# Weights of a quantised feed-forward prepared beside the attention's keys; the attention's tail and the feed-forward each in one run

## The chip, the cores and the metric

The kernel runs on one core of a Trainium2 chip. The time is that of the device for one execution, in microseconds (us). Engines: PE (TensorE), DVE (VectorE), ACT (ScalarE), POOL (GpSimd), and SP, which issues the DMAs.

## What is computed

`x` has 16 x 128 tokens of 256 elements. It passes through four layers, each an attention on a second sequence and a feed-forward; the change is in layer 2:

```python
x = x + tanh(g_xattn[2]) * L2_xattn(layernorm(x), ctx, Wq, bq, Wkv, bkv, Wp, bp)
x = x + tanh(g_ffn[2])   * L2_ffn(layernorm(x), W1, b1, W2, b2, s_act1, s_act2)

# L2_xattn: 16 heads of 16; q, k quantised to +-127 per head and token, v per channel over all tokens
#   (scale sv = max|v| / 127); p = softmax(q k^T) quantised to 0..255 per row; out = (p v) @ Wp + bp
# L2_ffn: W1 is 1024 x 256, W2 is 256 x 1024
sw1, sw2 = max|W1| / 7, max|W2| / 7
x_q  = clip(round(x / s1), -8, 7) * s1
W_q  = clip(round(W / sw), -8, 7) * sw        # for W1 and W2
b1_q, b2_q = round(b1 / (s1*sw1)) * (s1*sw1), round(b2 / (s2*sw2)) * (s2*sw2)
h_q  = clip(round(relu(x_q @ W1_q^T + b1_q) / s2), 0, 15) * s2
out  = h_q @ W2_q^T + b2_q
```

## The kernel before

Everything stays in SBUF: `X` and `H` hold the residual and its normalised form, 128 tokens by 16 tiles (t) by 256; `hT` holds the transposed form. The layers are written one behind the other. Within a layer each engine has its own program, and the engines meet at semaphores only; between layers all engines meet at a barrier. An engine works its program in order, so whatever stands behind a wait waits too. Rounding is done by adding and subtracting a large constant, MAGIC.

The quantised attention, `quantised_attention`, has four parts.

1. `run(NormTransposed, LoadSplit)`, 1281 to 1308: layer norm and transposition of x, and the split of the context and of the weights wq, wk, wv and wp into an f16 high and low part (ACT copies, DVE subtracts, L1034 and L1039).
2. A block for keys, values and queries, 1308 to 1413. SP issues four small loads (biases); DVE waits for all of them. PE projects 16 key tiles into two PSUM banks, and DVE adds the bias in tile after tile (L2068). POOL adds gate x bp to all of X in one instruction (L1953). Then PE projects the values, which ACT evacuates (L2020), while DVE makes the keys' integers; then the queries in the same way (L2075), the values' integers, and the queries' integers, with transpositions by PE and ACT between. The value scales `sv`, one for each of the 256 channels, lie across partitions; SP writes them to DRAM and reads them back in broadcast form as `svb`.
3. The main loop over 256 pairs of a tile and a head, 1413 to 2173: scores on PE, maxima on DVE, exp on ACT, a DMA transposition, a cast on POOL, the weighted sum on PE. It leaves unscaled outputs in `H` and the row sums in `sums`.
4. The tail. `Transposed` with `ScaledOutputs`: DVE sums, takes the reciprocal and, for each pair of tiles, multiplies by it (L2267), multiplies by `svb` (L2274) and subtracts the high part (L461); ACT makes the high part and copies; PE transposes in f16 (L502); ACT and DVE evacuate. When all of it is done `OutProjection` runs: six matmuls of 256 columns for a tile, two banks, and DVE adds each tile to X (L2301).

The feed-forward, `quantised_ffn`, has two blocks. In the first SP loads both weights, 1 MB each, and the small vectors; DVE does the layer norm (L94 to L104), the largest magnitudes of both weights (L2396), the input's integers (L2401 to L2403), the scales and biases (L2405 to L2417), and the weights' integers in three passes each (L2420 to L2422). POOL takes the maximum across partitions (L2380) and adds gate x b2 to X (L2382). PE and ACT transpose the integers. In the second block, four times for 512 tokens: eight times a hidden product (L2438), ReLU with scale and bias on ACT (L2468), rounding in two steps on DVE (L2489, L2491) with two buffers each; when all eight are there, 32 matmuls for the output (L2454) and two additions to X on DVE (L2479).

Of the kernel before, what the change touches and what calls it, by code (L numbers as in the profile page):

```python
# [14 lines left out]
P = 128  # L15
NB = 16
# [1868 lines left out]
def quantised_attention(nc, sh, a, gate):  # L1885
# [13 lines left out]
    with ExitStack() as ctx:  # L1899
# [11 lines left out]
        svb = sb("svb", [P, D])  # L1911
# [3 lines left out]
        with ExitStack() as inner:  # L1915
            cT = sb("cT", [P, 2, KT * T], F16, inner)
            wq, wk, wv = (sb(x, [P, 2, KT * D], F16, inner) for x in ("wq", "wk", "wv"))
            with ExitStack() as head:
                items = [(cT, a["ctxT"]), (wq, a["qa_wq"]), (wk, a["qa_wk"]), (wv, a["qa_wv"]), (wp, a["qa_wp"])]
                run(nc, NormTransposed(nc, head, sh, "qa_hT"), LoadSplit(nc, head, items, "qa_load"))  # L1920
            Y = sb("Y", [P, NB, D], F32, inner)
            Z = sb("Z", [P, NB, D], F32, inner)
            stack = sb("stack", [P, NB, NH, SLOT], F16, inner)
            ints = sb("ints", [P, KT, T], BF16, inner)
            amax = sb("amax", [P, NB, NH], F32, inner)
            sv = sb("sv", [P, KT], F32, inner)
            rsv = sb("rsv", [P, KT], F32, inner)
            s_b, s_b4, s_mmk, s_mmq, s_mmv, s_evk, s_evq, s_evv, s_c, s_st, s_st1, s_st2, s_vi, s_Tk, s_Tq, s_Tv, s_tk, s_tq, s_tv, s_sv, s_out, s_in = map(sem, (
                "bias", "b4", "mmk", "mmq", "mmv", "evk", "evq", "evv", "chain", "st", "st1", "st2", "vi", "Tk", "Tq", "Tv", "tk", "tq", "tv", "sv", "svout", "svin"))
# [3 lines left out]
            sv_dram = nc.dram_tensor("qa_value_scales", [P, KT], F32, kind="Internal").ap()  # L1933
# [4 lines left out]
            with nc.Block() as block:  # L1938
                @block.sync
                def _(sp):  # L1940
# [64 lines left out]
                def _(act):  # L2005
# [9 lines left out]
                    act.wait_ge(s_b, 64)  # L2015
# [13 lines left out]
                    transposed(KT, lambda t: V[:, t, :].rearrange("p (m c) -> p m c", m=KT), s_Tv, s_tv)  # L2029
                    act.wait_ge(s_st1, 1)  # L2030
# [5 lines left out]
                def _(dve):  # L2036
# [27 lines left out]
                    dve.wait_ge(s_b, 64)  # L2064
# [181 lines left out]
class ScaledOutputs:  # L2246
# [29 lines left out]
    def scalar(self, act):  # L2276
        pass
# [1008 lines left out]
```

## Time and profile before

| | |
|---|---|
| three runs | 2568.63, 2575.75, 2576.99 us; median 2575.75 |
| the profiled execution | 2577.9 us |
| its span (first to last instruction) | 2576.2 us |
| head of the attention (norm, split) | 1281 to 1308 |
| keys, values, queries | 1308 to 1413 |
| main loop | 1413 to 2173 |
| tail | 2173.6 to 2214.8 |
| feed-forward, preparation | 2216.1 to 2261.0 |
| feed-forward, products | 2261.0 to 2312.6 |
| next layer's attention | 2313 to 2471 |
| next layer's ternary feed-forward | 2471.4 to the end |

All times of the profile are us from the start of the span. A row of a stretch gives how long each engine was busy in it and how many instructions began there; PEclk is the clock that PE was granted, as a share of 2.4 GHz, so 0.50 is the lower of its two levels, 1.2 GHz. A row of a group takes together the instructions of one line, engine and shape. PE's ends are modelled, and a busy PE need not be one at its peak.

### The profile page before, as it was taken

The numbers are of one execution on the slowest core, as the hardware profiler recorded it, in microseconds if no ns is written. First come the engines' busy times: TensorE is split into PE (matmuls) and PEld (weight loads), VectorE is DVE, ScalarE is ACT, GpSimd is POOL, SyncE is SP. The second block draws the span as 40 slices with busy tenths as digits, with TensorE's granted clock in tenths as the row PEclk, the third lists the DMA queues.
The fourth block names the chain that finished last, engine by engine and source line by source line (L and its number), as shares of the span: only waits on it lengthen the run. The fifth ranks groups of instructions, "written<-read, shape, count | busy, mean of one in ns | idle before, by whom it ended". The sixth has DMA issues, their size and how long they took to land. (4 is left out here: it accounts for less than half of the span.)

```text
span 2576.2 us, 51573 instructions
## 1 busy us (share of the span) xinstructions
PE 2065.3 (80%) x17553; PEld 1136.7 (44%) x17553; DVE 1827.0 (71%) x3580; ACT 1523.3 (59%) x2785; POOL 888.5 (34%) x795
## 2 busy tenths in 40 slices
PE   4867999999978868999756788888888885357856
PEld 1334656555645635887433233333333332224433
DVE  4776755555555587333565999999999998866865
ACT  3455533333356755333334899999999997144555
POOL 4730000000015523001310667777777774105401
PEclk8778999999989979999866555555555555687989
DMA  6351222222240072322200454554444443001101
GB/s 194 84 222 61 68 66 66 65 69 65 66 134 27 3 270 58 67 67 63 79 22 2 78 91 91 91 92 93 92 91 91 91 93 64 35 20 47 28 1 34
DMA packets 384505, 195.75 MB, mean 76 GB/s; under 512 B 312443, under 2 KB 355835, under 8 KB 382203
## 3 DMA queue, kind: packets, MB, share of 16 engines
q1 hardware_dynamic: 381245, 184.87, 28.9%
q0 software_dynamic: 3072, 8.39, 1.0%
q8 instruction: 116, 1.90, 0.3%
q14 instruction: 72, 0.59, 0.1%
HBM read 95.38 MB, written 23.09 MB: 46 GB/s over the span
## 5 line engine op out<-in xcount | busy, mean ns | idle before, releaser
L2212 ACT ACTIVATE qa_e<-qa_S,qa_nb,qa_sq 128x512 uint8<-128x512 f32 (+1 forms) x805 | 710.5, 892 | 15.1 <-DVE qa_nb L2227 9.0
L2223 DVE TENSOR_REDUCE qa_mx<-qa_S 128x1 f32<-128x512 f32 x1024 | 637.2, 683 | 25.7 <-PE qa_S L2178 23.1
L2178 PE MATMUL qa_S<-qa_kT,qa_qb 128*128 128x512 f16 x1024 | 536.5, 612 | 114.3 <-ACT qa_e L2212 102.9
L2154 POOL CAST qa_pT<-qa_eT 128x2048 bf16<-128x2048 uint8 x256 | 483.7, 1892 | 210.4 <-DMA qa_eT<-qa_e 157.9
L2178 PEld LDWEIGHTS qa_S<-qa_kT,qa_qb 128*128 128x128 f16 x1024 | 89.9, 106 | 455.9 <-ACT qa_e L2212 440.6
L1116 POOL MEMSET rms_nothing<- 128x512 f16 x1 | 0.5, 524 | 580.3 <-POOLq L3177 580.3
L973 PE MATMUL moe_G<-hT,moe_W 128*128 (+1 forms) x792 | 193.8, 381 | 7.1 <-DVE moe_zero L941 7.1
L982 PE MATMUL moe_O<-moe_W,moe_ap 128*128 (+1 forms) x1584 | 194.5, 273 | 4.1 <-DVE moe_ap L937 4.1
L913 ACT ACTIVATE moe_ap<-moe_a 128x512 f16<-128x512 f32 x132 | 83.4, 632 | 193.4 <-DVE moe_a L935 193.4
L2187 PEld LDWEIGHTS qa_O<-qa_V,qa_pT 128*128 128x128 bf16 x4096 | 162.4, 107 | 75.0 <-issue 67.1
L973 PE MATMUL moe_U<-hT,moe_W 128*128 (+1 forms) x792 | 193.0, 380 | 0.0
L982 PEld LDWEIGHTS moe_O<-moe_W,moe_ap 128*128 128x128 f16 x1584 | 154.7, 98 | 50.4 <-DVE moe_ap L937 3.9
L932 DVE TENSOR_TENSOR moe_t<-moe_sg,moe_wb 128x512 f32<-128x512 f32 x132 | 91.4, 693 | 111.8 <-ACT moe_sg L908 107.3
L2187 PE MATMUL qa_O<-qa_V,qa_pT 128*128 128x16 bf16 x4096 | 158.0, 177 | 7.1 <-POOL qa_pT L2154 7.1
L2212 ACT ACTIVATION_READ_ACCUMULATOR qa_e<-qa_S,qa_nb,qa_sq 128x1 f32 x805 | 161.1, 200 | 0.0
L908 ACT ACTIVATE moe_sg<-moe_G 128x512 f32<-128x512 f32 x132 | 78.9, 598 | 132.3 <-PE moe_G L973 132.1
L937 DVE TENSOR_TENSOR moe_ap<-moe_a,moe_ap 128x512 f16<-128x512 f32 x132 | 91.4, 693 | 92.0 <-ACT moe_ap L913 92.0
L1704 DVE TENSOR_TENSOR moe_a<-moe_GU,moe_sg 128x512 f32<-128x512 f32 x78 | 53.9, 690 | 116.1 <-PE moe_GU L1779 88.0
L1779 PE MATMUL moe_GU<-moe_xs,moe_W 128*128 128x256 f16 x1104 | 130.0, 275 | 5.0 <-issue 5.0
L1588 ACT ACTIVATE moe_ap<-moe_a 128x512 f16<-128x512 f32 x78 | 49.3, 632 | 121.8 <-DVE moe_a L1704 115.5
L973 PEld LDWEIGHTS moe_U<-hT,moe_W 128*128 (+1 forms) x792 | 77.7, 98 | 94.1 <-issue 1.3
L1779 PEld LDWEIGHTS moe_GU<-moe_xs,moe_W 128*128 x1104 | 109.0, 99 | 18.6 <-issue 5.2
(432 smaller groups left out, 3433.7 us busy)
## 6 DMA issues: line engine op xcount, KB each, us to landing
moe_wb<-weights_T SPq DMA_DIRECT2D x264, 128.0 KB, 2.8
moe_W<-in_moe_w SPq DMA_DIRECT2D x40, 384.0 KB, 11.3
moe_W<-in_moe_w SPq DMA_DIRECT2D x11, 1152.0 KB, 14.8
moe_xs_rows<-rms_nothing SPq DMA_DIRECT2D x46, 128.0 KB, 1.9
moe_ys_rows<-moe_ys SPq DMA_DIRECT2D x23, 256.0 KB, 2.1
conv_rows<-conv_parts SPq DMA_DIRECT2D x16, 256.0 KB, 3.4
qa_eT<-qa_e SPq DMA_TRANSPOSE x256, 3.0
conv_qst<-conv_rows SPq DMA_DIRECT2D x96, 32.0 KB
```

Of the source, the lines that this page charges most:

```text
L908: nc.scalar.activation(sg[:, u, :], G[:, u, :], ACT.Silu).then_inc(s_sg[u], 1)
L913: nc.scalar.activation(ap[:, u, 0, :], a[:, u, :], ACT.Copy).then_inc(s_hi[u], 1)
L932: nc.vector.tensor_tensor(t1[:, u, :], sg[:, u, :], wb[:, u, :], ALU.mult).then_inc(s_t1[u], 1)
L937: nc.vector.tensor_tensor(ap[:, u, 1, :], a[:, u, :], ap[:, u, 0, :], ALU.subtract).then_inc(s_lo[u], 1)
L973: last = nc.tensor.matmul(X_[:, u, :], sh.W[:, f, wp, base + k * P:base + (k + 1) * P], sh.hT[:, xp, k, bass.ds(c * CT, CT)], start=i == 0 ...
L982: last = nc.tensor.matmul(O[:, t, :], ap[:, u, xp, t * P:(t + 1) * P], sh.W[:, f, wp, 4 * P:TW], start=False, stop=False, skip_group_check ...
L1779: last = nc.tensor.matmul(out[:, half * SLOT_TILE:(half + 1) * SLOT_TILE], W[:, bass.ds(f, 1), wp, base + k * P:base + (k + 1) * P], xs[:, ...
L2154: nc.gpsimd.tensor_copy(pT[:, u % RING, :, :].rearrange("p (b r) q -> p b r q", r=2), pairs).then_inc(s_cast, 1)
L2178: nc.tensor.matmul(S[:, bank(m), :], qb[:, g // 2, j, g % 2, :], kT[:, g, q * QW:(q + 1) * QW], start=True, stop=True).then_inc(s_S, 1)
L2187: last = nc.tensor.matmul(O[:, h * HD:(h + 1) * HD], pT[:, u % RING, b, :], V[:, b, h * HD:(h + 1) * HD], start=b == 0, stop=b == NB - 1)
L2212: nc.scalar.activation(e8[:, u % RING, q * QW:(q + n) * QW], S[:, b:b + n, :].rearrange("p b c -> p (b c)"), ACT.Exp, bias=nb[:, u % 2:u % ...
L2223: nc.vector.reduce_max(mx[:, i, q:q + 1], S[:, bank(m + q), :], axis=AXX).then_inc(s_mx, 1)
```

## The change

The weights of the feed-forward get a class of their own, `QuantisedWeights`, whose buffers live through both layers. SP loads them in the attention's second block, behind one more load, `wpf`, the f32 output weights, which `LoadSplit` no longer takes. DVE works on the feed-forward's weights in pieces between the evacuations of the key tiles: magnitudes behind tiles 1 and 2, scales behind 5, the three passes of W1 behind 6 to 8 and of W2 behind 9 to 11, b1 and b2 behind 12 and 13. POOL takes their maximum behind its addition to X. The value scales are multiplied into the rows of `wpf` (there each channel is a partition), and the high and low part of `wp` are made from that; `svb` and its way through DRAM are gone.

The tail becomes one block, `scaled_projection`: POOL multiplies the tiles by the reciprocals, PE transposes pairs in f32, ACT makes the high part from PSUM and DVE the low part, PE projects, DVE adds a pair to X at once; transposes run two pairs ahead of projections.

`quantised_ffn` becomes one block: statistics by quarters of four tiles, ACT normalises with 1/s1 in the scale, DVE makes the integers of a quarter in two operations, and 32 steps of a hidden product (two ahead), ReLU, rounding and that product's four matmuls to the output. b2 enters PSUM by f32 matmuls of one row of ones with `b2`, in place of the addition on POOL. All loops are written out. The diff, cut:

```diff
+    def greatest(self, pool):
+        pool.wait_ge(self.s_am, 2)
+        self.nc.gpsimd.partition_all_reduce(self.amx[:, :], self.am[:, :], P, bass.bass_isa.ReduceOp.max).then_inc(self.s_amx, 1)
...
+    def magnitudes(self, dve, i):
+        if i == 0:
+            dve.wait_ge(self.s_load, 96)
+        self.nc.vector.tensor_reduce(out=self.am[:, i:i + 1], in_=(self.f1, self.f2)[i][:, :], axis=AXX, op=ALU.max,
+                                     apply_absolute_value=True).then_inc(self.s_am, 1)
...
+    def divided(self, dve, i):
+        f = (self.f1, self.f2)[i]
+        self.chained(self.nc.vector.tensor_scalar(f[:, :], f[:, :], self.rsw[:, i:i + 1], MAGIC, ALU.mult, ALU.add))
+    def rounded(self, dve, i):
+        f = (self.f1, self.f2)[i]
+        self.chained(self.nc.vector.tensor_scalar(f[:, :], f[:, :], MAGIC, 7.0, ALU.subtract, ALU.min))
+    def integers(self, dve, i):
+        f, w = (self.f1, self.f2)[i], (self.w1, self.w2)[i]
+        self.nc.vector.tensor_scalar(w[:, :], f[:, :], -8.0, None, ALU.max).then_inc(self.s_w, 1)
...
-                    sp.wait_ge(s_sv, 1)
-                    sp.dma_start(sv_dram, sv[:, :]).then_inc(s_out, 16)
-                    sp.wait_ge(s_out, 16)
-                    sp.dma_start(svb[:, :], sv_dram.rearrange("p m -> (p m)").partition_broadcast(P)).then_inc(s_in, 16)
-                    sp.wait_ge(s_in, 16)
+                    sp.dma_start(wpf[:, :], a["qa_wp"]).then_inc(s_b, 16)
+                    next_weights.load(sp)
...
+                    next_weights.greatest(pool)
...
+                    act.wait_ge(s_wps, KT)
+                    nc.scalar.activation(wp[:, 0, :], wpf[:, :], ACT.Copy).then_inc(s_wphi, 1)
...
-                    dve.wait_ge(s_b, 64)
+                    dve.wait_ge(s_b, 80)
...
+                    next_weights.start(dve)
+                    for t in range(NB):
+                        dve.wait_ge(s_mmk, t + 1)
+                        nc.vector.tensor_tensor(Y[:, t, :], QP[:, t % 2, 0:D], bias[:, 1, :], ALU.add).then_inc(s_evk, 1)
+                        if t in (1, 2):
+                            next_weights.magnitudes(dve, t - 1)
+                        if t == 5:
+                            next_weights.scales(dve, next_gate)
+                        if t in (6, 9):
+                            next_weights.divided(dve, (t - 6) // 3)
+                        if t in (7, 10):
+                            next_weights.rounded(dve, (t - 7) // 3)
+                        if t in (8, 11):
+                            next_weights.integers(dve, (t - 8) // 3)
+                        if t == 12:
+                            next_weights.hidden_bias(dve)
+                        if t == 13:
+                            next_weights.output_bias(dve)
+                    dve.wait_ge(s_evk, NB + 2)
...
+                    for m in range(KT):
+                        nc.vector.tensor_scalar(wpf[:, m * D:(m + 1) * D], wpf[:, m * D:(m + 1) * D], sv[:, m:m + 1], None, ALU.mult).then_inc(s_wps, 1)
...
+                    dve.wait_ge(s_wphi, 1)
+                    nc.vector.tensor_tensor(wp[:, 1, :], wpf[:, :], wp[:, 0, :], ALU.subtract)
...
+            @block.gpsimd
+            def _(pool):
+                pool.wait_ge(s_inv, 1)
+                for t in range(NB):
+                    h = sh.H[:, t, :].rearrange("p (h d) -> p h d", h=heads)
+                    nc.gpsimd.tensor_tensor(h, h, inv[:, t, :].unsqueeze(2).to_broadcast([P, heads, D // heads]), ALU.mult).then_inc(s_scaled, 1)
...
+                def low(p):
+                    dve.wait_ge(s_hi, p + 1)
+                    nc.vector.tensor_tensor(target(1, p), turned(p), target(0, p), ALU.subtract).then_inc(s_lo, 1)
...
+                nc.vector.reciprocal(inv[:, :, :].rearrange("p t h -> p (t h)"), tot[:, :]).then_inc(s_inv, 1)
+                low(0)
+                low(1)
+                for p in range(PAIRS):
+                    if p + 2 < PAIRS:
+                        low(p + 2)
+                    residual(p)
...
+                def transposes(p):
+                    pe.wait_ge(s_scaled, 2 * p + 2)
+                    if p >= 3:
+                        pe.wait_ge(s_lo, p - 2)
...
+                def project(p):
+                    pe.wait_ge(s_lo, p + 1)
+                    if p >= 3:
+                        pe.wait_ge(s_res, p - 2)
...
+                transposes(0)
+                transposes(1)
+                for p in range(PAIRS):
+                    if p + 2 < PAIRS:
+                        transposes(p + 2)
+                    project(p)
...
+                def hidden(n):
+                    q, f = divmod(n, NF)
+                    pe.wait_ge(s_hT, q + 1)
+                    if n >= RING:
+                        pe.wait_ge(s_r, n - RING + 1)
...
+                def biases(q):
+                    if q >= 2:
+                        pe.wait_ge(s_res, 2 * (q - 1))
+                    for i in range(Q):
+                        nc.tensor.matmul(O[:, q % 2, i, :], ones[0:1, :], b2[0:1, :], start=i % 2 == 0, stop=False, skip_group_check=True)
+                def down(n):
+                    q, f = divmod(n, NF)
+                    pe.wait_ge(s_hq, n + 1)
+                    for i in range(Q):
+                        last = nc.tensor.matmul(O[:, q % 2, i, :], hq[:, n % 4, i * P:(i + 1) * P], w2[:, f * D:(f + 1) * D],
+                                                start=False, stop=f == NF - 1, skip_group_check=True)
+                    last.then_inc(s_D, 1)
...
+                tokens(0)
+                hidden(0)
+                hidden(1)
+                biases(0)
+                for n in range(NQ * NF):
+                    q, f = divmod(n, NF)
+                    if f == 2 and q + 1 < NQ:
+                        tokens(q + 1)
+                    if f == 5 and q + 1 < NQ:
+                        biases(q + 1)
+                    if n + 2 < NQ * NF:
+                        hidden(n + 2)
+                    down(n)
...
+                for q in range(NQ):
+                    deviations(q)
+                    if q < 2:
+                        for t in range(q * Q, (q + 1) * Q):
+                            normalise(t)
+                tokens(0)
+                for n in range(NQ * NF):
+                    q, f = divmod(n, NF)
+                    if f == 3 and q + 1 < NQ:
+                        tokens(q + 1)
+                    relu(n)
+                    if f % 2 == 0 and q + 2 < NQ:
+                        normalise((q + 2) * Q + f // 2)
...
+                def rounded(n):
+                    dve.wait_ge(s_r, n + 1)
+                    nc.vector.tensor_scalar(z[:, n % 2, :], r[:, n % RING, :], 15.0, MAGIC, ALU.min, ALU.add).then_inc(s_z, 1)
+                    dve.wait_ge(s_z, n + 1)
+                    if n >= 4:
+                        dve.wait_ge(s_D, n - 3)
+                    nc.vector.tensor_scalar(hq[:, n % 4, :], z[:, n % 2, :], MAGIC, None, ALU.subtract).then_inc(s_hq, 1)
...
+                statistics(0)
+                statistics(1)
+                scales(0)
+                statistics(2)
+                scales(1)
+                integers(0)
+                statistics(3)
+                scales(2)
+                scales(3)
+                for n in range(NQ * NF):
+                    q, f = divmod(n, NF)
+                    rounded(n)
+                    if f == 0 and q + 1 < NQ:
+                        integers(q + 1)
+                    if f == 3 and q:
+                        output(q - 1)
+                output(NQ - 1)
```

## Rows read from the trace of the kernel before

**Rows 1.** Stretches: length, busy us (instructions) per engine, clock, DMA share, GB/s

```profile
1313.20:1328.40 15.20, 13.43 (x88) 9.23 (x89) 7.24 (x18) 0.00 (x0) 8.84 (x1) 0.78 0.01 1
1328.40:1355.70 27.30, 11.14 (x58) 5.44 (x56) 26.66 (x11) 5.51 (x8) 0.00 (x0) 0.78 0.00 0
...
1369.80:1397.70 27.90, 15.79 (x94) 9.42 (x93) 27.49 (x15) 16.87 (x33) 0.00 (x0) 0.58 0.07 5
1413.00:2173.00 760.00, 638.50 (x5126) 228.61 (x5125) 722.72 (x1552) 730.67 (x1614) 536.66 (x386) 0.51 0.48 90
2173.60:2199.40 25.80, 8.26 (x64) 6.17 (x64) 22.85 (x58) 10.03 (x24) 0.00 (x0) 0.50 0.00 0
2199.40:2214.80 15.40, 14.05 (x96) 9.47 (x96) 7.74 (x16) 0.00 (x0) 0.00 (x0) 0.86 0.00 0
2216.10:2261.00 44.90, 6.24 (x32) 3.33 (x32) 42.58 (x75) 7.34 (x18) 12.14 (x2) 0.52 0.14 50
2261.00:2312.60 51.60, 37.85 (x192) 18.31 (x192) 30.99 (x72) 24.05 (x32) 0.00 (x0) 0.89 0.00 0
```

**Rows 2.** Groups, 2216 to 2261: count | busy us, mean ns | idle

```profile
L2421 DVE TENSOR_SCALAR qf_f<-qf_f 128x2048 f32<-128x2048 f32 x2 | 10.9, 5474 | 0.1
L2382 POOL TENSOR_TENSOR X<-X,qf_b 128x4096 f32<-128x4096 f32 x1 | 9.8, 9774 | 8.1 <-DVE qf_b L2417 8.1
...
L2396 DVE TENSOR_REDUCE qf_am<-qf_f 128x1 f32<-128x2048 f32 x2 | 4.5, 2281 | 0.0
...
L2420 DVE TENSOR_SCALAR qf_f<-qf_f,qf_rsw 128x2048 f32<-128x2048 f32 x2 | 2.6, 1280 | 0.0
...
L2380 POOL PARTITION_ALL_REDUCE qf_amx<-qf_am x1 | 2.4, 2369 | 61.7 <-DVE qf_am L2396 61.7
...
L2413 DVE TENSOR_SCALAR qf_b<-qf_b,qf_c 128x256 f32<-128x256 f32 x1 | 0.4, 354 | 0.0
```

**Rows 3.** Order in time, DVE at the keys: start us, duration

```profile
1313.26 0.29 DVE L2065 TENSOR_SCALAR qa_bias<-qa_bias 128x256 f32<-128x256 f32 x1 [5.61 <-DMA qa_bv<-in_qa_bv]
```

**Rows 4.** Groups of the stretch from 1281 to 1308

```profile
L584 ACT ACTIVATE H<-X,qa_hT_shift,qa_hT_rstd 128x256 f32<-128x256 f32 x16 | 8.3, 594 | 0.0
...
L560 DVE TENSOR_TENSOR hT<-qa_hT_TP,hT 128x512 f16<-128x512 f32 x8 | 5.1, 686 | 3.4 <-ACT hT L589 3.3
...
L589 ACT ACTIVATE hT<-qa_hT_TP 128x512 f16<-128x512 f32 x8 | 4.1, 587 | 0.0
...
L1039 DVE TENSOR_TENSOR qa_wp<-qa_load_stage,qa_wp 128x512 f16<-128x512 f32 x1 | 0.7, 687 | 0.0
```

**Rows 5.** DMA issues, 2214 to 2232: count, KB each, us to landing

```profile
qf_sa<-in_qf_s SPq DMA_DIRECT2D x2, 0.5 KB, 6.0
```

**Rows 6.** Groups of the stretch from 2173 to 2215

```profile
L2260 DVE RECIPROCAL qa_inv<-qa_tot 128x256 f32<-128x256 f32 x1 | 1.8, 1753 | 0.0
```

**Rows 7.** Groups of POOL, whole span

```profile
L2987 POOL TENSOR_TENSOR X<-X,tf_tmp 128x256 f32<-128x256 f32 x16 | 11.8, 739 | 89.0 <-DVE tf_tmp L3143 89.0
```

**Rows 8.** Stretches around changes of the clock, columns as in rows 1

```profile
1286.00:1291.00 5.00, 4.20 (x16) 2.85 (x16) 4.19 (x21) 5.00 (x13) 0.00 (x0) 0.50 0.87 351
2199.00:2204.00 5.00, 4.56 (x23) 3.29 (x24) 1.36 (x3) 0.00 (x0) 0.00 (x0) 0.51 0.00 0
...
2520.00:2540.00 20.00, 13.20 (x94) 7.58 (x92) 14.86 (x31) 13.25 (x13) 3.01 (x4) 0.91 0.08 27
```

**Rows 9.** Groups of the stretch from 2261 to 2313

```profile
L2468 ACT ACTIVATE qf_r<-qf_H,qf_b,qf_c 128x512 f32<-128x512 f32 x32 | 24.1, 778 | 32.2 <-PE qf_H L2438 31.8
...
L2489 DVE TENSOR_SCALAR qf_z<-qf_r 128x512 f32<-128x512 f32 x32 | 13.5, 422 | 4.0 <-ACT qf_r L2468 4.0
L2479 DVE SCALAR_TENSOR_TENSOR X<-qf_O,qf_c,X 128x512 f32 x8 | 6.0, 751 | 16.2 <-PE qf_O L2454 16.2
```

**Rows 10.** Order in time, ternary feed-forward's first product and copy

```profile
2483.87 1.00 ACT L3053 ACTIVATE hT<-tf_TI 128x1024 f16<-128x1024 f16 x1
...
2484.93 5.30 PE L3007 MATMUL tf_H<-tf_w,hT 128*128 128x512 f16 x12 [1.94 <-ACT hT L3053]
```

More of the change, by code:

```diff
@@ L2431, in quantised_ffn, with quarter, _, tokens @@
+        def quarter(q):
+            return slice(q * Q, (q + 1) * Q)
         with nc.Block() as block:
+            @block.gpsimd
+            def _(pool):
+                nc.gpsimd.memset(ones[:, :], 1.0).then_inc(s_ones, 1)
             @block.tensor
             def _(pe):
-                def hidden(ch, f):
-                    n = ch * NF + f
-                    pe.wait_ge(s_r, n + 1)
+                def tokens(q):
+                    pe.wait_ge(s_ints, q + 1)
+                    if q:
+                        pe.wait_ge(s_hT, q)
+                    for i in range(Q):
+                        for k in range(KT):
+                            last = nc.tensor.transpose(TI[:, k, i, :], ints[:, q * Q + i, k * P:(k + 1) * P], sh.identh[:, :])
+                    last.then_inc(s_TI, 1)
+                def hidden(n):
[3 more added lines that the diff above has]
+                        pe.wait_ge(s_r, n - RING + 1)
@@ L2437, in hidden @@
                     for k in range(KT):
[L2438 to L2439 removed]
+                        last = nc.tensor.matmul(Hp[:, n % RING, :], w1[:, k * weights.F + f * P:k * weights.F + (f + 1) * P],
+                                                sh.hT[:, 0, k, q * CT:(q + 1) * CT], start=k == 0, stop=k == KT - 1)
@@ L2458, in _, with deviations @@
             @block.scalar
             def _(act):
-                act.sem_inc(s_r, 2)
-                with act.Fori(0, T // CT // 2) as pair:
-                    for par in range(2):
-                        ch = pair * 2 + par
-                        for f in range(NF):
-                            n = ch * NF + f
-                            act.wait_ge(s_H, n + 1)
-                            act.wait_ge(s_z, n + 1)
-                            nc.scalar.activation(r[:, f % 2, :], Hp[:, f % 2, :], ACT.Relu, bias=b1[:, f:f + 1], scale=c[:, 4:5]).then_inc(s_r, 1)
+                def deviations(q):
+                    act.wait_ge(s_mv, (q + 1) * Q)
+                    nc.scalar.activation(std[:, quarter(q)], mv[:, quarter(q), 1], ACT.Sqrt, bias=sh.eps[:, 0:1]).then_inc(s_std, 1)
@@ new lines, in scales @@
+                def scales(q):
+                    dve.wait_ge(s_std, q + 1)
+                    nc.vector.reciprocal(rstd[:, quarter(q)], std[:, quarter(q)]).then_inc(s_rstd, 1)
+                    dve.wait_ge(s_rstd, q + 1)
+                    nc.vector.tensor_scalar(scale[:, quarter(q)], rstd[:, quarter(q)], weights.rsa[:, 0:1], None, ALU.mult).then_inc(s_scale, 1)
+                    dve.wait_ge(s_scale, q + 1)
+                    nc.vector.scalar_tensor_tensor(out=shift[:, quarter(q)], in0=mv[:, quarter(q), 0], scalar=-1.0, in1=scale[:, quarter(q)],
+                                                   op0=ALU.mult, op1=ALU.mult).then_inc(s_shift, 1)
@@ new lines, in output @@
+                def output(q):
+                    dve.wait_ge(s_O, q + 1)
+                    for pair in range(2):
+                        xs = sh.X[:, q * Q + 2 * pair:q * Q + 2 * pair + 2, :]
+                        nc.vector.scalar_tensor_tensor(out=xs, in0=O[:, q % 2, 2 * pair:2 * pair + 2, :], scalar=c[:, 5:6], in1=xs, op0=ALU.mult,
+                                                       op1=ALU.add).then_inc(s_res, 1)
+                statistics(0)
+                statistics(1)
+                scales(0)
```

349 lines of the change are left out of this document (158 added, 191 removed).

## The prediction

> **What bounds the kernel now.** I read four views in this order: the busy time by stretch, the groups of instructions of the stretches that the change touches, their order in time, and the granted clock around them. The stretches first [rows 1]. The attention's main loop (1413 to 2173) is 760 us long with ACT busy 730.7 of them; nothing in it is edited, so what counts is what stands before and behind it. Before it DVE is the bound: from 1328.4 to 1355.7 it works 26.66 of 27.3 us, from 1369.8 to 1397.7 it works 27.49 of 27.9. Between 1313.2 and 1328.4, while the keys are projected, it works only 7.24 of 15.2, and PE 13.43. Behind the loop DVE works 22.85 of 25.8 us (scaling, splitting, transposing the outputs), and then PE 14.05 of 15.4 (the output projection): one after the other. In the feed-forward's preparation (2216.1 to 2261.0) DVE works 42.58 of 44.9 us; in its product loop (to 2312.6) PE shows 37.85, DVE 30.99 and ACT 24.05 of 51.6, again in turns: no engine is the bound, the alternation is. The reader is to see four stretches in which one engine works and the others wait.
>
> **1. Weights quantised beside the keys.** In the preparation DVE spends on the weights two reductions of 2.28 us, two divisions of 1.28, two clippings of which one took 9.7 us (10.9 for the two) and two conversions like the divisions [rows 2]. The long clipping stands next to POOL's addition of b2 to X, 9.77 us in one instruction [rows 2]; without that neighbour it costs 1.2. In the new place these are 4.6 + 6 x 1.26 = 12.1 us, the seven small operations of the scales and four for b1, which I estimate at 0.2 each, below the 0.35 of a 128x256 one [rows 2] (2.3), and three of that size for b2 (1.0): 15.4 us of DVE. They are put between the evacuations of the key tiles, where DVE idles 8 us, but they do not fit: 7.2 + 15.4 = 22.6 us of DVE work against a stretch of 15.2. Three waits are added on DVE. It starts behind the load of bv, after an idle 5.61 us [rows 3]; now it waits for one more load, wpf, issued behind bv. This block starts 0.6 us earlier, since the split of wp (0.69 us, such ones start every 0.6) leaves the one ahead [rows 4]; the extra load takes about 1.0 more, so DVE starts at 1313.7. In tile 1 it waits for all six loads of the feed-forward. In the old place the last landed 6.0 us after its issue [rows 5], which is 8.6 us after the first issue; here the first is issued near 1309.7, behind 256 KB more, so the last lands near 1318.9, and DVE, ready at 1315.3, stands 3.6 us. Behind it wait the key evacuations, and behind these PE, which has only two banks. At tile 5 DVE waits for POOL's maximum (2.37 us [rows 2]), which POOL does only after its 8.84 us on X [rows 1] and after both reductions: about 0.5 us, and PE's next tile about 1. Sum: 1313.7 + 22.6 + 3.6 + 1.5 = 1341.4 instead of 1328.4, **+13.0 us**. All of it moves the end, since DVE is full behind it; the value projection and its evacuation on PE and ACT only move along, and the scores of DVE's next stretch are long enough to cover them. Bounds: +8 if the loads are there in time and the gaps hide more, +17 if a late load holds each tile.
>
> A rule fits the 9.7 us. The Trainium skill (SBUF — State Buffer, "SBUF: two separate sides") says that VectorE in a two-port mode and GpSimd take a shared pair of ports for a whole instruction and block each other. By it the new divisions would be blocked if they met POOL's 8.84 us on X; that runs near 1314 to 1323 and they start near 1327, so by my times they just miss it. The trace agrees as far as the clipping goes.
>
> **2. Value scales in the output weights.** Two multiplications of 128x256 are added on DVE ahead of the values' integers, 0.3 each, near the b2 operation's 0.35 [rows 2]: **+0.6 us**, in a stretch where DVE is full. ACT's copy of wpf (0.6) stands where ACT waits for the query integers, the low part (0.69, as the wp split [rows 4]) behind DVE's last integers, beside ACT's copy of the stack: nothing. The round trip of the scales through DRAM was beside other work and gives nothing back. If that cover is gone they cost 1.3. Bounds 0 and +1.3.
>
> **3. The tail as one pipeline.** Before: 41.2 us from 2173.6 to 2214.8. The row sums (1024 elements, half of a 2.28 us reduction) and the reciprocal of 1.75 [rows 6] stay, 3.1 us with their hand-over. POOL then scales each tile; the nearest row is its 128x256 addition, 739 ns [rows 7], so a pair each 1.5 us. PE transposes a pair with four f32 transposes: 16 of them kept it busy 4.20 us at the low clock [rows 8], so 1.05 a pair there and about 0.55 at the high one. ACT copies (0.59), DVE subtracts (0.69 [rows 4]) and later adds the pair (0.75 [rows 9]): 1.45 us of DVE a pair. The projection is 12 matmuls: before, 96 filled 15.4 us with the clock rising on the way [rows 1], which is 2.56 us a pair at the low level and 1.35 at the high one. So PE is the bound: 3.6 us a pair low, 1.9 high. The first projection starts after 3.1 + 1.5 + 1.05 + 0.6 + 0.7 = 7 us. The clock: in the old projection PE was at 0.51 (1.2 GHz) for 5 us of dense work [rows 8]; the mean of 0.86 over the 15.4 us [rows 1] puts the rest at 1.0 (2.4 GHz). Taking the same delay plus some for the transposes among them, 2.5 pairs low and 5.5 high make 19.5: the tail is 26.5 us long, **-14.7 us**. Bounds: 24 us (a rise at once) and 35 us (none; the first transposes run ahead).
>
> A rule speaks against this. f32 transposes at 4.20 busy of 5.00 us left the clock at 0.50 [rows 8]; the Trainium skill (TensorE: Matmul & The Clock Gate, "Part 4: PE-mode transpose") says transposes do not count as PE-busy in the same way. With them at 29% of PE's time in the new tail the rise may fail; that is a rival below.
>
> **4. The feed-forward in one run.** The old one takes 96.4 us. New head: statistics by quarters, ACT normalises with 1/s folded in, integers of the first quarter, transposes, first product. The ternary feed-forward behind is built so, and its first product starts at 2484.93 [rows 10], 13.6 us after its stretch began; it has a maximum more (1.2 us) and per-tile integers, and here ACT comes to its copy only behind the fourth deviations, so 11.5, and the first ReLU ends at 13.2. The loop has 32 steps. ACT: 0.78 a step [rows 9], plus 3 copies of 1.0 [rows 10] and 8 normalisations (16 took 8.3 us [rows 4]): 32 us. DVE: two operations of 0.42 a step [rows 9], which overlap a little (0.80), plus 3 pairs of integer operations (1.35) and 8 additions of 0.75: 36 us. PE at the high clock: 64 matmuls of 512 and 128 of 256 columns, which is 256 times the 0.11 us of the old projection at that level, 29 us; with 32 transposes and the sixteen bias matmuls 35. A bias matmul (f32, one row, 256 columns) has no row; two f32 transposes of 128 columns, 0.53 at the low level [rows 8], are the nearest, I take 0.5 low and 0.27 high; from nothing to 1.0 us each it moves the sum by -4 to +8, mostly beside DVE. So the three engines are level at 32 to 36 us, and coupled through three PSUM banks, three r and four hq buffers. I take 1.25 us a step (1.11 is DVE alone): 40 us, with 12.4 ahead of the first ReLU and 3.6 for the last products and additions: 56 us, **-40.4 us**. The b2 addition on POOL and its block on DVE are gone within this. The clock should hold: the ternary stretch, with PE busy 13.20 of 20 us, had 0.91 [rows 8]. Instructions for the unrolled loop I cost at nothing, as that stretch is unrolled too. Bounds for the stage: 51 (DVE alone) and 64 (1.5 us a step).
>
> **The sum** is made against the profiled execution, 2577.9 us (span 2576.2): +13.0 + 0.6 - 14.7 - 40.4 = -41.5, so 2536.4. The runs' median of 2575.75 lies 2.15 lower: 2534.
>
> **Rivals.**
> A. The tail stays at 1.2 GHz because of the transposes: 35 instead of 26.5 us, 2543. For it the 0.50 beside f32 transposes, against it that 71% of PE's time is projection.
> B. The loop's step is 1.5 us: DVE's in-order insertions (1.35 integers, 1.5 additions) empty the small rings and each costs PE and ACT a stall. Stage 64, 2542. For it: with two hidden products ahead, the way through ReLU (0.78) and two DVE operations (0.85) is as long as PE's work of two steps.
> C. The keys' stretch hides more than I count (+8): 2529.
> D. PE is kept at 1.2 GHz in the loop as well, by short stops: 16.5 us a quarter, stage 81, tail 35: 2534 + 25 + 8.5 = 2567.5. Against it the 0.91 of the ternary stretch.
> E. Slower: the feed-forward's steps run in series. PE's in-order queue waits at each down product for hq, and if the ring lets no product go ahead, a step is hidden 0.43 to 0.86, ReLU 0.78, two DVE operations 0.85, down 0.43 to 0.86, hand-overs 0.3: 2.8 us at the high level. The stage is then 105.5 us and the kernel 2583.5. It decides from 2.55 us a step: (56 + 41.5 - 16) / 32. For it the old loop's waits of PE; against it that hidden runs two steps ahead of down.
>
> **How the numbers follow.** Forecast 0.45; A 0.20; B 0.15; C 0.12; D 0.05; E 0.03. The range takes C with a better tail at the low end and A or B with a costly key stretch at the high one: 2520 to 2556; it leaves D, E and the far ends out. The likeliest case alone: 2526 to 2543. About 0.3% (7.7 us) is what a measurement of this kernel tells from no change. Faster by more: all but half of D, and E: 0.94; within: 0.03; slower: 0.03.
>
> **What would show it.** Step 1: the first reduction over Y starts about 13 us later from its block's start, DVE over 80% busy between, with one stop near 3.6 us at the first weight reduction. Step 2: no stop at the wp low part. Step 3: from the row sums to the last addition 26 us, clock near 1.0 in its second half. Step 4: the stage takes 56 us, clock above 0.9 from its second quarter, relu every 1.25 us. The prediction is wrong if the stage exceeds 70 us, the tail 35, or the main loop's 760 us move by more than 3.

## The result and the profile after

The changed kernel takes 2551.9 us (median of 6 runs, 2550.2 to 2560.8), the kernel before on the same chip 2576.8: ratio 0.9906, 95% interval 0.989 to 0.9922. That is 24.9 us less, against a forecast of 41.5. The profiled executions differ by 27.5 us (2550.38 against 2577.9; span 2548.7).

The stretches first (columns as in [rows 1]; they answer to its rows from 1313.2 on, and to the one from 2216 on):

```profile
1313.40:1343.10 29.70, 18.12 (x89) 10.68 (x90) 20.68 (x40) 0.00 (x0) 9.19 (x2) 0.61 0.15 60
1413.00:2187.00 774.00, 647.17 (x5184) 235.10 (x5184) 722.31 (x1553) 740.51 (x1628) 536.88 (x386) 0.51 0.49 88
2187.50:2200.00 12.50, 4.36 (x18) 3.19 (x19) 4.71 (x5) 1.79 (x3) 5.70 (x10) 0.50 0.00 0
2200.00:2213.20 13.20, 12.30 (x112) 10.95 (x109) 9.76 (x14) 2.98 (x5) 3.61 (x7) 0.99 0.01 1
2214.20:2225.60 11.40, 1.01 (x8) 0.78 (x8) 10.10 (x46) 7.31 (x14) 0.19 (x1) 0.63 0.00 0
2225.60:2283.50 57.90, 45.99 (x248) 26.32 (x248) 35.12 (x78) 30.67 (x43) 0.00 (x0) 0.90 0.00 1
```

The reduction behind the keys starts at 1343.1 instead of 1328.5 (+14.7; forecast +13.0). The row sums start 13.9 us later than before (2187.52 against 2173.63), so what lies between that reduction and them became under 1 us shorter in all (ACT's exponentials 709.3 us, before 710.5). The tail lasts 25.6 us (-15.5; forecast -14.7). The feed-forward, head 11.4 and loop 57.9, lasts 69.3 us (-27.1; forecast -40.4). The miss of 13 us is in that last row. Counted to the last addition of the stage the kernel is 29.0 us ahead (2283.5 against 2312.5); the layers behind it, which are not edited, took 1.5 us longer.

VectorE beside the keys, in order of time (start, duration, idle time ahead and its releaser):

```profile
1319.14 2.29 DVE L1935 TENSOR_REDUCE qf_am<-qf_f 128x1 f32<-128x2048 f32 x1 [4.48 <-DMA qf_sa<-in_qf_s]
...
1329.00 0.17 DVE L1942 TENSOR_SCALAR qf_sw<-qf_amx 128x2 f32<-128x2 f32 x1 [2.59 <-POOL qf_amx L1927]
...
1330.53 1.28 DVE L1965 TENSOR_SCALAR qf_f<-qf_f,qf_rsw 128x2048 f32<-128x2048 f32 x1
...
1332.18 1.22 DVE L1969 TENSOR_SCALAR qf_f<-qf_f 128x2048 f32<-128x2048 f32 x1
```

GpSimd at the same place and in the tail:

```profile
1314.09 8.82 POOL L2041 TENSOR_TENSOR X<-X,qa_bias 128x4096 f32<-128x4096 f32 x1 [58.46 <-DVE qa_bias L2157]
1328.52 0.37 POOL L1927 PARTITION_ALL_REDUCE qf_amx<-qf_am  x1 [5.62 <-issue]
...
2194.30 9.31 POOL L2385 TENSOR_TENSOR H<-H,qa_inv 128x256 f32<-128x256 f32 x16 [8.21 <-issue]
```

VectorE stops twice for long, 4.5 us for the loads and 2.6 us for the scales (and 1.3 us for a key tile from TensorE). The second stop is GpSimd's: its maximum needs data that were ready at 1324.0 and starts 4.6 us after that; "issue" says that it waited for nothing recorded. The tail has the same gap: the reciprocals are ready at 2190.5, the first scaling starts at 2194.3.

The groups of the feed-forward's stretch (count | busy us, mean ns | idle ahead and its releasers), which answer to [rows 9]:

```profile
L2568 ACT ACTIVATE qf_r<-qf_H,qf_b,qf_c 128x512 f32<-128x512 f32 x32 | 24.4, 777 | 19.7 <-PE qf_H L2512 17.3 <-DVE qf_z L2610 1.8
L2526 PE MATMUL qf_O<-qf_w,qf_hq 128*128 128x256 f16 x128 | 21.0, 291 | 9.4 <-DVE qf_hq L2614 9.2
...
L2610 DVE TENSOR_SCALAR qf_z<-qf_r 128x512 f32<-128x512 f32 x32 | 13.6, 424 | 21.0 <-ACT qf_r L2568 20.7
L2520 PE MATMUL qf_O<-qf_b,qf_ones 1*128 1x256 f32 x32 | 9.7, 453 | 0.0
```

The ReLU still waits 17.3 us for hidden products (31.8 before). From first to last ReLU there are 52.9 us for 31 steps, 1.71 each, not 1.25. The bias matmuls are 16 in the code and 32 in the trace: each f32 product is split in two. How they hold up the rest is seen on PE and ACT at the first quarter:

```profile
2225.61 1.89 PE L2512 MATMUL qf_H<-hT,qf_w 128*128 128x512 f16 x4 [1.86 <-ACT hT L2560]
2227.43 3.78 PE L2520 MATMUL qf_O<-qf_b,qf_ones 1*128 1x256 f32 x8
2231.14 1.03 PE L2512 MATMUL qf_H<-hT,qf_w 128*128 128x512 f16 x2
```

```profile
2227.86 0.77 ACT L2568 ACTIVATE qf_r<-qf_H,qf_b,qf_c 128x512 f32<-128x512 f32 x1
2232.21 0.78 ACT L2568 ACTIVATE qf_r<-qf_H,qf_b,qf_c 128x512 f32<-128x512 f32 x1 [3.59 <-PE qf_H L2512]
```

Four bias matmuls take 3.78 us at the low clock (0.95 each), and the third hidden product stands behind them in TensorE's order, with the ReLU behind it.

A second kind of wait is TensorE's own, 9.2 us for rounded hidden units (`qf_hq`, in the groups above). The first of them, on ACT and then on PE:

```profile
2235.09 1.02 ACT L2560 ACTIVATE hT<-qf_TI 128x1024 f16<-128x1024 f16 x1 [1.61 <-PE qf_TI L2503]
...
2237.76 0.61 PE L2526 MATMUL qf_O<-qf_w,qf_hq 128*128 128x256 f16 x4 [1.41 <-DVE qf_hq L2614]
```

ACT works in order: the copy of the next quarter's transposed tokens stands ahead of a ReLU whose hidden product is already there, so that ReLU, its rounding and its down product come late. Each of the three such copies is followed by a wait of 1.41 us, 4.2 in all; VectorE's additions to X are followed by three of 1.07, its integer operations by 0.62 and 0.47, and the last by 0.63.

### The profile page after: what moved, and what is told of

The parts are those of the page before. It is cut to its first block and busy times, and to the rows that moved or that the text cites. A ratio compares the mean times of both kernels' runs of the same rounds, so it can differ in the third digit from the quotient of the medians.

```text
span 2548.7 us, 50934 instructions
## 1 busy us (share of the span) xinstructions
PE 2066.7 (81%) x17553; PEld 1141.6 (45%) x17553; DVE 1796.1 (70%) x3525; ACT 1521.6 (60%) x2776; POOL 888.3 (35%) x811
## 5 line engine op out<-in xcount | busy, mean ns | idle before, releaser
L2325 ACT ACTIVATE qa_e<-qa_S,qa_nb,qa_sq 128x512 uint8<-128x512 f32 (+1 forms) x805 | 709.3, 891 | 15.6 <-DVE qa_nb L2340 9.0
## 6 DMA issues: line engine op xcount, KB each, us to landing
moe_W<-in_moe_w SPq DMA_DIRECT2D x40, 384.0 KB, 11.5
```

Source lines behind the costliest of these rows:

```text
L2325: nc.scalar.activation(e8[:, u % RING, q * QW:(q + n) * QW], S[:, b:b + n, :].rearrange("p b c -> p (b c)"), ACT.Exp, bias=nb[:, u % 2:u % ...
```

## Experiments

The stages, in us, to within 0.1. Keys: from the scaling of the bias to the first reduction over Y. Tail: from the row sums to the feed-forward's first statistics. Feed-forward: from there to the end of the last addition. Ratio: to the kernel before on the same chip. Each is the changed kernel with the edit named; e6 and e9 contain e5's, e7 contains e4's, e10 those of e4, e6 and e9.

| kernel | keys | tail | feed-forward | ratio, 95% interval |
|---|---|---|---|---|
| before | 15.2 | 42.6 | 96.4 | 1 |
| changed | 29.7 | 26.7 | 69.3 | 0.9906 (0.989 to 0.9922) |
| e1 no bias matmul | 30.0 | 27.0 | 58.9 | 0.9874 (one run) |
| e2 f16 bias | 29.7 | 27.1 | 65.1 | 0.9881 (0.9865 to 0.9898) |
| e3 down later | 29.7 | 27.6 | 64.7 | 0.9881 (one run) |
| e4 both | 29.8 | 27.2 | 54.1 | 0.9846 (0.983 to 0.9862) |
| e5 maximum first | 35.8 | 23.9 | 73.5 | 0.9926 (0.9899 to 0.9953) |
| e6 e5, work later | 32.8 | 22.6 | 69.2 | 0.9898 (0.9874 to 0.9921) |
| e7 e4, PE kept busy | 29.8 | 27.3 | 54.1 | 0.983 (0.9811 to 0.985) |
| e8 move undone | 13.4 | 23.5 | 86.3 | 0.9919 (0.9893 to 0.9944) |
| e9 e5, addition later | 27.1 | 23.3 | 69.3 | 0.9893 (0.987 to 0.9915) |
| e10 together | 24.7 | 23.7 | 54.4 | 0.9802 (0.9782 to 0.9821) |
| e11 e10, PE kept busy | 24.7 | 23.2 | 54.2 | 0.9796 (0.9776 to 0.9816) |

**The loop: e1 to e4.** Theory 1 was the bias matmuls in TensorE's order, theory 2 the ring (a hidden product must pass ReLU and VectorE before TensorE, which looks only two products ahead, can go on), theory 3 TensorE's clock.

e1 (in `down` only the changed argument is shown):

```diff
-                    for i in range(Q):
-                        nc.tensor.matmul(O[:, q % 2, i, :], ones[0:1, :], b2[0:1, :], start=i % 2 == 0, ...)
-  (down)  start=False
+  (down)  start=f == 0 and i % 2 == 0
```

> Leaves out the second bias of the feed-forward: its 16 one-row f32 matmuls are gone, the output lacks b2. Stage in the changed kernel: 69.3 us from the end of the tail's block to the last residual addition, of which 11.4 go before the first hidden projection; forecast was 56. Theory 1 (the bias matmuls stand in TensorE's order ahead of hidden projections that ScalarE waits for; 9.7 us of TensorE time): the stage falls by 8 to 10 us, to 59 to 61, and ScalarE's waits of 3.6, 1.6 and 3.3 us for a hidden projection go. Theory 2 (the loop of projection, ReLU, two VectorE instructions and down projection is bound by its ring, not by TensorE's amount of work): it falls by less than 4 us, and the same waits of about 0.7 to 0.9 us a step stay. Theory 3 (TensorE's granted clock, low for the first 6 us and again for 4 us in the middle, is what costs): it falls by 4 us or less and the low stretches stay.

e2, `sel` being zero but for two rows of ones, `bh` the bias in a high and a low half:

```diff
-                        nc.tensor.matmul(O[:, q % 2, i, :], ones[0:1, :], b2[0:1, :], ...)
+                        nc.tensor.matmul(O[:, q % 2, i, :], sel[:, :], bh[:, :], ...)
```

> The same bias, but each of the 16 matmuls is one f16 product of 64 rows (a selector with two rows of ones, and the bias in a high and a low half), instead of one f32 product of a single row. Theory 1: a 256-column f16 matmul takes 0.11 to 0.22 us instead of 0.5 to 0.95, so 7 to 8 of the 9.7 us go and the stage falls from 69.3 to 61 or 62; the total time by 7 us, to about 2545. Theories 2 and 3: less than 4 us, total 2549 to 2552.

e3:

```diff
                     if n + 2 < NQ * NF:
                         hidden(n + 2)
-                    down(n)
+                    if n:
+                        down(n - 1)
+                down(NQ * NF - 1)
```

> TensorE issues the down projection of step n one step later, behind the hidden projection of n + 3, so that the two VectorE instructions have a step more; the bias matmuls stay. Theory 2 (TensorE waits 9 us for VectorE's rounded hidden units and hands the wait on to the next hidden projection): the stage falls by 5 us or more, to 64 or less. Theory 1: the bias matmuls stay where they are and what they hold up stays, 0 to 3 us fall. Theory 3: none, or slightly more if the clock stays up.

e4 has both edits.

> The f16 bias and the later down projection together. If theories 1 and 2 each hold a part, the gains add: stage 57 to 60 us, total about 2541 to 2543. If theory 1 alone holds, this equals the run with the f16 bias alone within 1 us; if theory 3 holds the stage stays over 65.

Measured against 69.3 us: e1 -10.4, e2 -4.2, e3 -4.6, e4 -15.2. Without the bias (e1) the stage loses as much as the bias's 9.7 us of TensorE time, and its clock stayed up in the middle as well: theory 1 holds at the size expected, less some 1.4 us that the clock gives (below). ACT's waits for hidden products fall from 17.3 to 5.7 us, but TensorE still waits 9.5 us for rounded units, which is theory 2's part. The f16 form makes the first four bias products 1.03 us instead of 3.78:

```profile
2215.97 1.03 PE L2527 MATMUL qf_O<-qf_bh,qf_sel 64*128 64x256 f16 x4
```

but the stage fell by only 4.2 of the 7 to 8 us that I expected. e3 is just short of its 5 us; TensorE's waits for rounded units fall there from 9.2 to 1.7 us, those behind ACT's copies as well as those behind VectorE's insertions. e4 is 3 us better than the 57 to 60 expected: in the stages the edits bring more than their sum, 15.2 against 8.8 us. In the whole time that is less clear: the ratios give about 6.4 us to each edit and 15.5 to both, with intervals some 4 us to either side, and e3 is one run. The stretches of the loop in e2, e3 and e4 show why:

```profile
2235.00:2241.00 6.00, 4.93 (x24) 2.38 (x22) 3.58 (x9) 2.65 (x5) 0.00 (x0) 0.72 0.00 0
...
2247.00:2256.00 9.00, 6.82 (x28) 3.35 (x29) 5.58 (x13) 3.79 (x6) 0.00 (x0) 0.66 0.01 2
```

```profile
2237.00:2244.00 7.00, 6.86 (x30) 4.22 (x31) 4.80 (x13) 3.17 (x6) 0.00 (x0) 0.76 0.00 0
...
2252.00:2257.00 5.00, 5.00 (x23) 2.71 (x23) 2.62 (x7) 2.33 (x3) 0.00 (x0) 0.66 0.01 2
```

```profile
2224.50:2234.00 9.50, 8.82 (x63) 5.28 (x62) 7.21 (x17) 8.63 (x14) 0.00 (x0) 1.00 0.01 3
2234.00:2244.00 10.00, 8.61 (x62) 5.10 (x61) 8.73 (x21) 7.79 (x12) 0.00 (x0) 1.00 0.00 0
2244.00:2254.00 10.00, 8.61 (x58) 5.08 (x57) 8.40 (x21) 7.61 (x11) 0.00 (x0) 1.00 0.00 1
```

In e2 and e3 the granted clock falls twice in the middle, in e4 (last fence) never. A share of 0.72 over 6 us is 3.4 us at 1.2 GHz; so counted, e2 has 9.5 us of it in the middle, e3 6.8, the changed kernel 3.4 (0.86 over 12 us), e4 none. What such a microsecond costs can be estimated from e5, whose feed-forward is the changed kernel's code: it had about 13.6 us of it, 10 more, and was 4.2 us longer, so 0.4 us each, from one pair of traces. Less that, the edits bring an estimated 6.6 (e2), 6.0 (e3) and 13.8 (e4): they nearly add. So theory 2 holds beside theory 1, with some 6 us, and theory 3 is real but small: an estimated 1.4 us for the low spell in the middle of the changed kernel, and 1.2 us for the one at the start of e4's loop (e7 below, against e4). The step of e4 is 36.8/31 = 1.19 us.

**GpSimd: e5, e6, e9.** Theory 4 is that GpSimd takes some 6 us to go from one kind of instruction to the other. e5:

```diff
+                    next_weights.greatest(pool)
                     pool.wait_ge(s_b4, 2)
                     nc.gpsimd.tensor_tensor(sh.X[:, :, :], sh.X[:, :, :], bias[:, 2, :]..., ALU.add)
-                    next_weights.greatest(pool)
```

> Beside the keys GpSimd takes the maximum over partitions first and adds the scaled bias to X after it, instead of the other way round; nothing else is changed. In the changed kernel GpSimd starts the maximum 5.6 us after the addition's end and the tail's first scaling 3.8 us after its reciprocals are ready, each time with a MODIFY_POOL_CONFIG on its queue and nothing recorded in between. Theory 4 (a switch between GpSimd's instruction sets costs 5.6 to 6.7 us each way): the first switch now lies under the transfers, the switch back in front of the addition to X, and none in the tail; the scales follow the magnitudes at once (-2.6 us beside the keys), the tail starts 3.8 us earlier (25.6 to about 22 us), total -6 us, about 2546 on the scale of the changed kernel's 2551.9. Rival (the time belongs to each instruction's own start, as the first of its kind in a block): the tail still starts 3.8 us late and only the 2.6 us or nothing is gained. A third thing that can go against it: the addition to X, 8.8 us, now lies beside the divisions on VectorE; if these slow down by more than 2.6 us in all, the keys' stretch is longer than before.

e6 also shifts the weights' work: `if t in (1, 2)` for the magnitudes becomes `if t in (4, 5)`, `t == 5` for the scales `t == 7`, the rest two tiles later.

> As the run with GpSimd's order swapped, and the weights' work starts behind key tile 4 instead of tile 1 (magnitudes at tiles 4 and 5, scales at 7, the rest at 8 to 15), so that VectorE evacuates tiles 2 to 4 while the weights are still arriving (4.5 us of waiting). If the wait is the cost, 1.5 to 3 us less between the start of the keys and the reduction behind them than with the order swapped alone (29.7 us in the changed kernel, about 27 with the swap, about 25 here). If TensorE's own pace of 0.9 us per tile sets the stretch, no difference.

e9 is e5 with one wait more ahead of the addition:

```diff
                     pool.wait_ge(s_b4, 2)
+                    pool.wait_ge(s_st, 1)
```

> As the run with GpSimd's order swapped, but the addition to X waits until VectorE has split the keys, and so lies beside the evacuation of the queries instead of beside the weights' divisions. In the swapped run one VectorE rounding pass of 1.22 us took 9.91 us, beginning with the addition's 8.79 us and ending with it; the keys' stretch was 35.8 us. Theory 5 (GpSimd's addition of two operands in SBUF keeps VectorE's fast one-operand pass from running): without it that pass is back at 1.2 us, the keys' stretch falls to 27.1 us (29.7 less the 2.6 us of waiting for the scales), the evacuations of the queries are not stretched by more than 1 us, and with the tail's 3.7 us the total is 5 to 6 us below the changed kernel: ratio about 0.9885. Rival (the pass waits for something else, for instance the transfer or the switch that stands in GpSimd's queue): the long pass stays, or comes back at another place, total as the swapped run, 0.9926.

In e5 the maximum comes 0.1 us after the magnitudes and the tail's first scaling 0.1 us after the reciprocals, so the late start belongs to the change of kind and not to the first instruction of a block; the tail is 2.8 us shorter. But the keys' stretch is 6.1 us longer, by one VectorE pass, and instead of the 6 us gained that were expected the ratio is higher than the changed kernel's, within the intervals. VectorE and then GpSimd in e5:

```profile
1335.60 1.22 DVE L1969 TENSOR_SCALAR qf_f<-qf_f 128x2048 f32<-128x2048 f32 x1
...
1337.19 9.91 DVE L1973 TENSOR_SCALAR qf_w<-qf_f 128x2048 f16<-128x2048 f32 x1
```

```profile
L2042 POOLq MODIFY_POOL_CONFIG  x2: 82/82/83, 1330.4 to 1330.4; - x2
L2042 POOL TENSOR_TENSOR X<-X,qa_bias x1: 8793/8793/8793, 1337.2 to 1337.2; 128x4096 f32<-128x4096 f32 x1
```

The pass begins with GpSimd's addition and ends 1.1 us after it. In e6 another pass met the addition (9.37 us for one of 1.22), in e9 none, and there the stretch is 27.1 us, the number expected; the addition ran at 1353 beside the evacuations of the queries, which kept their 0.42 us. This is what the Trainium skill (SBUF — State Buffer, "SBUF: two separate sides") says of the pair of ports that VectorE in a two-port mode and GpSimd share: the one holds it for its whole instruction and the other waits. The trace agrees, to the 1.1 us that the pass still takes once the addition has ended. The gap of 6.8 us between the configuration and the addition is the switch back: 1330.4 to 1337.2. Toward the maximum it was 5.6 us (1322.9 to 1328.5 in the changed kernel), near the "approximately 6 µs" that the Trainium skill (GPSIMD Engine Reference, "2.1 Instruction dispatch") gives for a freshly loaded kernel's first call; the way back costs the same here. e6 and e10 gain 2.4 us, within the 1.5 to 3 expected, by evacuating three tiles under the loads (27.1 to 24.7; in e5 and e6 after taking off the 8.7 and 8.2 us of the blocked pass).

**The move: e8.** The weights' code stands in the feed-forward's head, behind the statistics, the loads at its start:

```diff
-                    next_weights.load(sp)                    (keys; so for all of next_weights there)
+                weights.load(sp)                             (feed-forward)
+                weights.magnitudes(dve, 0)                   (behind scales(3); then all that follows)
+                pe.wait_ge(weights.s_w, 1)                   (ahead of hidden(0); 2 ahead of biases(0))
```

> Undoes the move of the weights' quantisation: nothing of it beside the keys, all of it (loads, magnitudes, maximum, divisions, biases) in the head of the fused feed-forward, behind the layer norm's statistics. Work on VectorE: about 15.5 us (two magnitudes 4.6, scales 1.2, six passes 7.4, biases 1.9, of which the second matrix's 4.8 can lie beside the first hidden projections), loads of 2 MB in about 10 us beside the statistics. Theory A (the move only changes the place): the keys' stretch loses 14.7 us and the stage gains 12 to 16, the tail starts 3.8 us earlier since no maximum stands before it; total 2545 to 2552, that is the same as the changed kernel or up to 6 us better. Theory B (what the prediction assumed: the work beside the keys is cheaper, since part of it lies beside TensorE): the stage gains 18 us or more, total 2555 or more.

Keys -16.3, tail -3.2, feed-forward +17.0: -2.5 us by the stages, while the ratio is 0.0013 (3 us) higher; the intervals overlap, so no difference is shown. The +17.0 lies between the two theories (12 to 16, and 18 or more), but e8's loop also had more time at 1.2 GHz (0.85 over its last 35 us, 10.5 us of it against 3.4), an estimated 3 us; without that it is in theory A's range. So the move as it was made gained nothing. Beside the keys VectorE works 20.68 of the 29.7 us and stops for 8.4 (4.5 for the loads, 2.6 for GpSimd's maximum, 1.3 for a tile): as much as the 8 us of idle time that the work was moved into. No wait for the loads remains in e8 (the statistics cover them).

The move does better once those stops are mended: the three stages add up to 125.7 us in the changed kernel, 123.2 in e8, 119.7 in e9 and 117.2 with e10's keys and e9's other two. By the ratios e9 is 0.9893 against e8's 0.9919, intervals overlapping, so that is shown in the traces only, and e8's form could be mended too (TensorE waits 2.9 us there for the second weights' integers, ahead of its bias matmuls).

**TensorE kept busy: e7, e11.** The added lines of e7 are these; e11 is e10 with 24 in place of 36, none behind `tokens(0)`, and 8 such matmuls ahead of the tail's first transposes.

```diff
+                for _ in range(36):
+                    nc.tensor.matmul(Hp[:, 2, :], sh.identh[:, :], w1[:, 0:CT], start=True, stop=True)
                 tokens(0)
+                (4 more)
```

> As the run with the f16 bias and the later down projection, and TensorE fills its 10.7 us of waiting ahead of the feed-forward's first transposes with 36 matmuls that nobody reads, and 4 more behind them. Theory 3 (the granted clock at the loop's start costs): the loop starts at 1.00 instead of 0.50, the first ReLU comes no earlier (VectorE's statistics set it) or 0.3 us earlier, and the first 4 us of low clock fall away: stage 54.1 to about 52 us. Against it: if more activity brings the clock down within the 40 us of the loop, as it did in the middle of the changed kernel and twice with either edit alone, the stage is 54 to 58.

> As the run before it, with TensorE given 24 matmuls ahead of the feed-forward's first transposes and 8 ahead of the tail's, all unread. With 36 and 4 the loop took 40.5 instead of 41.7 us but began 1.2 us later, as the extra matmuls outlasted the wait. With 24 the first ReLU is back at +12.4 us or earlier and the stage at 52.5 to 53.5; in the tail the first two pairs run at 1.00 instead of 0.50: 1 to 2 us less. Total 2 to 3 us below the run before it. If the granted clock is spent sooner for it, no gain or a loss of some us.

e7's loop ran at 1.00 throughout, 40.5 us instead of 41.7 (e4), but the first ReLU came 1.2 us later: the stage is e4's, 54.1 instead of the 52 expected, and the ratio's interval overlaps e4's. In e11 they ended too early (at 2201.4; the loop starts at 2205.6, with only eight transposes between):

```profile
2194.20:2203.00 8.80, 5.71 (x31) 2.63 (x32) 7.88 (x34) 5.55 (x11) 1.59 (x5) 1.00 0.00 0
2203.00:2205.60 2.60, 0.26 (x5) 0.09 (x2) 2.21 (x13) 1.76 (x4) 0.00 (x0) 0.76 0.00 0
2205.60:2211.00 5.40, 5.39 (x17) 2.12 (x18) 3.37 (x8) 3.20 (x5) 0.00 (x0) 0.50 0.00 0
```

The clock was 1.00 during them and 0.50 when the loop began. The stage stayed at 54.2, not the 52.5 to 53.5 expected, and the tail fell by some 0.4 us instead of 1 to 2: the clock was 1.00 behind the 8 matmuls, from 2174 on, and 0.50 again when the first projection came at 2178.5. A number between 24 and 36 was not tried.

**All together: e10.**

> The f16 bias, the later down projection, GpSimd's maximum first with the addition beside the queries, and the weights' work from key tile 4 on. By the stages: keys 24.7 us (32.8 less the 8.1 that one pass lost), tail from the row sums to the next stage 22.6 to 24, feed-forward 54.1. Against the changed kernel -5.0, -3 to -4 and -15.2: -23 us, ratio about 0.982 to 0.981. If the clock falls in the loop, 3 to 5 us more.

All three stages came as expected, 24.7, 23.7 and 54.4. The ratio is 0.9802, so 51 us below the kernel before and an estimated 27 below the changed one, where the stages and the forecast give 23. e11 is the same within its interval.

## Why the prediction was right and wrong

The direction, the four terms' signs and the range held; the size did not. That the range held is in part luck: the feed-forward's 69.3 us lie outside the bounds given for it (51 to 64) and just inside the 70 us named as the sign of being wrong, the total is 4 us below the range's upper end, and in the keys and in the tail errors of opposite sign cancelled.

1. Keys, +13.0, measured +14.7. The start (1313.7, measured 1313.4) and the divisions' escape from GpSimd's addition held: they ran 1.2 to 1.3 us each, and e5 shows the 8.7 us that the rule would have cost one of them. The nearness is again two errors. VectorE's work was put too high (22.6 us, measured 20.68), so that it was busy 70% of the stretch and not over 80%. The stops were put too low, 5.1 us against 8.4: the one for the loads at 3.6 (measured 4.5) and above all the one for the maximum at 0.5, measured 2.6, since GpSimd first switches. Before, the switch stood at 2215.8, hidden under an idle of 61.7 us [rows 2].
2. Value scales, +0.6: measured 0.62. The rest of that block was as much shorter (the first exponential of the main loop starts 14.65 us later, the reduction behind the keys 14.66), so it does not show in the total.
3. Tail, -14.7, measured -15.5, by two errors that cancel. GpSimd began 3.8 us late, which is the switch back, shown by e5, e8 and e9, where no maximum stands right ahead and the tail is 2.8 to 3.5 us shorter. The clock rose after about one pair instead of 2.5, and a pair then took 1.75 us instead of 1.9. Rival A is wrong: f32 transposes among the projections did not keep the clock down (0.99 from 2200 on), so the rule on transposes that spoke against this term did not bear on it here.
4. Feed-forward, -40.4, measured -27.1. The head was right: first product at +11.4 (11.5), first ReLU at +12.5 (12.4). The step that failed is "I take 1.25 us a step", by its treatment of the bias matmuls. I had them at 0.27 us (high) and 0.5 (low) and "mostly beside DVE"; they took 0.5 (1.99 us for four) and 0.95, and lay on the path, as each set of four stands ahead of a hidden product. Shown: e1's 10.4 us, some 9 without the clock's part. The rest, an estimated 6 us with e3, is rival B's mechanism: two hidden products ahead are as long as the way through ReLU and VectorE, so that each insertion is handed on; that argument stood in the prediction and got 0.15. It named only VectorE's insertions. ACT's three copies, which the sum had as 3 us of ACT's work and no wait, hold up as much: 4.2 of TensorE's 9.2 us. No run takes these two apart. The bias and the ring together are more than 13.3 us because the clean loop steps at 1.19, below the 1.25 assumed. The forecast of 56 us was right for a loop without these two faults (54.1).

## What to carry to other kernels

In an unrolled loop on an in-order engine, cost each inserted instruction as if all behind it waited, unless the queues behind are deeper than its duration; a f32 matmul of one row is no small one. Ask of each GpSimd instruction which one stands ahead of it: a change between the maximum over partitions and ordinary arithmetic cost 5.6 to 6.8 us here, free only under a wait. Moving work to a place with idle time gains only if the idle time is still there when its loads and helpers are counted: e8 undid such a move, and no loss could be measured.

## What the runs showed of the hardware

- An f32 matmul of 1 row and 256 columns is recorded as two, 0.95 us for the pair at 0.50 of the clock and 0.5 at 1.00; as one f16 product of 64 rows it took 0.26 at the low one.
- A VectorE pass of 1.22 us took 9.91 and 9.37 us when GpSimd's addition of two SBUF operands started with it; the two reductions and the evacuations from PSUM that met such an addition in the changed kernel were not lengthened (2.28 us, 0.42 us), nor the evacuations of the queries in e9 (0.42 us).
- The same feed-forward code took 69.2, 69.3, 69.3 and 73.5 us, the last with some 10 us more at 1.2 GHz. What brings the clock down in the loop stays open: it fell after stretches with TensorE at half its time or less in e2, but not in e1, which had the same.
